# A two-layer graph network on one core: eight units of the adjacency loaded ahead, fourteen moved by transposing DMA, reloads issued from SP

## What is computed

```python
h = relu(layernorm(x))
support = relu(quant(h) @ quant(weight_norm))
x = x + adj @ quant(support)                 # first layer ("layer 0")
h = relu(layernorm(x))
A = (adj + adj.T) * 0.5 + I
dinv = rowsum(A) ** -0.5                     # 0 where the sum is not positive
y = adj @ (dinv[:, None] * A * dinv[None, :])
x = x + y @ h                                # second layer
```

## Time and profile before

| | us |
|---|---|
| median of 3 runs | 505.09 (504.79 to 523.74) |
| the profiled execution, its own time | 509.47 |
| span of that execution, first to last instruction | 507.7 |
| TensorE busy in the span | 489.5 (96%) |
| VectorE, ScalarE, GpSimd busy | 275.9, 142.7, 36.5 |
| mean granted TensorE clock | 0.997 |

### The profile page before, as it was taken

One profiled execution on the slowest core, in us unless ns is written; L12 is line 12 of the kernel. 1 busy time (PEld: TensorE's weight loads), 2 busy tenths in 40 slices (PEclk: granted clock), 3 DMA queues, 4 the chain that ended last, 5 costly groups with the idle time before them and its releaser, 6 DMA issues.

```text
span 507.7 us, 6439 instructions
## 1 busy us (share of the span) xinstructions
PE 489.5 (96%) x2446; PEld 242.4 (48%) x2446; DVE 275.9 (54%) x368; ACT 142.7 (28%) x199; POOL 36.5 (7%) x51
## 2 busy tenths in 40 slices
PE   1899999997999999999999999999999999999997
PEld 1756555553564444444444444444444444444446
DVE  4964779896979878787798767450001000100000
ACT  1885852434544153444432121240000000000000
POOL 1325511132000000000000000000000000000000
PEclk9999999998999999999999999999999999999999
DMA  8970577999934043323224332018001000010001
GB/s 293 402 298 1 187 167 207 196 168 211 305 117 146 0 125 105 102 94 113 83 83 126 104 103 83 0 48 304 21 22 41 21 21 21 21 41 21 21 21 43
DMA packets 39948, 56.89 MB, mean 112 GB/s; under 512 B 22904, under 2 KB 23160, under 8 KB 39928
## 3 DMA queue, kind: packets, MB, share of 16 engines
q1 hardware_dynamic: 37040, 46.15, 30.6%
q10 hardware_dynamic: 2888, 10.49, 7.4%
HBM read 42.99 MB, written 8.39 MB: 101 GB/s over the span
## 4 chain that ended last, share of the span: by engine, by line
PE 84%; DVE 7%; DMA 4%; ACT 2%; issue 1%; SPq 1%; POOL 0%; ACTq 0%
PE ps_a L1098 31%; PE ps_p L997 14%; PE ps_p L1061 7%; PE ps_a L1061 7%; PE ps_b L1061 7%; PE ps_m L1061 4%; PE ps_h L1061 4%; DMA feat<-in_x 2%; DMA at<-at 2%; PE ps_b L979 1%; PE ps_b L951 1%; PE ps_m L997 1%; PE ps_h L997 1%; PE ps_a L979 1%; DVE at L801 1%; DVE small L849 1%
## 5 line engine op out<-in xcount | busy, mean ns | idle before, releaser
L997 PE MATMUL ps_p<-small,at 128*128 128x512 f16 x448 | 102.6, 384 | 2.8 <-DMA at<-at 2.8
L920 DVE SCALAR_TENSOR_TENSOR feat<-ps_a,feat 128x512 f32<-128x512 f32 (+1 forms) x16 | 10.8, 675 | 148.7 <-PE ps_a L1098 144.2
L1098 PE MATMUL ps_a<-small,at 128*128 128x512 f16 x360 | 80.1, 379 | 0.0
L1098 PE MATMUL ps_a<-a_in,at 128*128 128x512 f16 x360 | 80.1, 379 | 0.0
L997 PEld LDWEIGHTS ps_p<-small,at 128*128 128x128 f16 x448 | 44.1, 99 | 52.2 <-issue 5.6
L499 ACT ACTIVATE split<-a_in 128x1024 f16<-128x1024 f32 x30 | 31.7, 1057 | 101.8 <-PE ps_p L1061 90.0
L1098 PEld LDWEIGHTS ps_a<-a_in,at 128*128 (+1 forms) x360 | 35.2, 98 | 42.5
L1098 PEld LDWEIGHTS ps_a<-small,at 128*128 (+1 forms) x360 | 35.2, 98 | 42.5
L845 DVE TENSOR_TENSOR split<-a_in,split 128x1024 f16<-128x1024 f32 x30 | 36.7, 1225 | 34.0 <-ACT split L499 34.0
L1061 PE MATMUL ps_p<-feat,split 128*128 (+1 forms) x180 | 43.9, 379 | 0.5 <-DVE small L849 0.5
L1061 PE MATMUL ps_a<-feat,split 128*128 (+1 forms) x180 | 43.7, 379 | 0.0
(11 more groups left out here) (178 smaller groups left out, 445.0 us busy)
## 6 DMA issues: line engine op xcount, KB each, us to landing
a_in<-in_adj SPq DMA_DIRECT2D x34, 512.0 KB, 3.7
a_in<-in_adj ACTq DMA_DIRECT2D x20, 512.0 KB, 5.0
out<-feat SPq DMA_DIRECT2D x31, 256.0 KB, 2.5
feat<-in_x SPq DMA_DIRECT2D x8, 512.0 KB, 11.3
at<-in_adj SPq DMA_DIRECT2D x8, 512.0 KB, 14.1
feat<-out SPq DMA_DIRECT2D x4, 1024.0 KB, 9.6
at<-in_L_gnn_weight SPq DMA_DIRECT2D x2, 512.0 KB, 3.8
split<-in_adj SPq DMA_DIRECT2D x1, 512.0 KB, 15.8
```

The lines of the kernel that those rows point to most:

```text
L920: nc.vector.scalar_tensor_tensor(out, products, 1.0 / (SA * SZ), out, ALU.mult, ALU.add).then_inc(y_out, 1)
L997: last = nc.tensor.matmul(l0_bank(r), at_block(r, lo, j), small[:, j * D:(j + 1) * D], start=(j == 0 and lo == 0), stop=(j == T - 1 and lo ...
L1098: last = nc.tensor.matmul(BANK[n], at_block(t, lo, j), z_part(j, z_lo), start=(j == 0 and lo + z_lo == 0), stop=(j == T - 1 and lo == 1))
```

## The change

- `MOVED` becomes the fourteen odd units from 3 to 29. Units 3, 5, 27 and 29 are no longer turned. `ADDED` is 1 and these fourteen. Unit 29 gets a stage of its own place in tile 15.
- `AHEAD` becomes 20. Units 12 to 19 are loaded ahead into tiles 10 to 13 of `at`: 16 and 17 into tile 12 once the row transposes are done, 18, 19, 12 and 13 into tiles 13 and 10 once the support products are done, 14 and 15 into tile 11 once the support clamps are done. The ring of `a_in` starts again with unit 20.
- SP issues all loads of `adj`. ScalarE issues none.
- Moves run one step further ahead: step 1 moves units 7 and 9, step `r` from 2 to 11 moves unit `2r + 7`; units 3 and 5 are moved ahead of step 1. Writing a tile from 6 to 13 of `at` now waits until the two units that were loaded into it are done with (`waited_in`), in `move`, `hi_turned` and `lo_turned`.
- The row sums of units 0, 1, 2 and 4 come earlier on ScalarE. GpSimd's first addition waits for `hT_ready` instead of `sq_ready`.

The core of the diff:

```diff
-AHEAD = 12
+AHEAD = 20
-MOVED = tuple(range(7, 26, 2))
-ADDED = (1, 3) + MOVED
+MOVED = tuple(range(3, 30, 2))
+ADDED = (1,) + MOVED
...
         def stage(u, lo):
+            if u == 29:
+                return late(15, 2048 + lo * W, W, f16)
...
+        def in_tile(u):
+            return u // 2 + 4
+        def waited_in(u):
+            return 2 * (u // 2) - 8, 2 * (u // 2) - 7
         def unit_in(u):
             if RING <= u < AHEAD:
-                return late((9, 8, 7, 6)[(u - RING) // 2], u % 2 * 2 * W, W, f32)
+                return late(in_tile(u), u % 2 * 2 * W, W, f32)
...
-        TURNS = {r: [2 * r + 4] for r in range(2, 11)}
-        TURNS.update({1: [4, 5, 6], 11: [26, 27], 12: [28, 29, "acc"], 13: [30, 31]})
-        ROW_SUMS = {4: [0, 1], 5: [2, 3], 6: [4, 5], 8: [6, 8], "acc": []}
-        MOVES = {r: [2 * r + 5] for r in range(1, 11)}
+        TURNS = {r: [2 * r + 4] for r in range(2, 12)}
+        TURNS.update({1: [4, 6], 12: [28, "acc"], 13: [30, 31]})
+        ROW_SUMS = {2: [0, 1], 4: [2, 4], "acc": []}
+        MOVES = {r: [2 * r + 7] for r in range(2, 12)}
+        MOVES[1] = [7, 9]
...
             def move(u):
                 for lo, ready in ((0, hi_ready), (1, lo_ready)):
                     sp.wait_ge(ready, MOVED.index(u) + 1)
-                    if u == 13:
-                        free_slot(sp, 10 + lo)
+                    if u == 29:
+                        wait_moved(sp, 25)
+                        wait_moved(sp, 27)
+                    elif u >= 12:
+                        free_slot(waited_in(u)[lo])
...
-            for u in range(2, AHEAD):
-                rows(sp, u)
+            for u in range(2, 12):
+                rows(u)
             sums(0)
             sums(1)
+            sp.wait_ge(hT_ps, T // 2)
+            rows(16)
+            rows(17)
+            move(3)
+            sp.wait_ge(sup_ps, T // 2)
+            for u in (18, 19, 12, 13):
+                rows(u)
+            sp.wait_ge(sq_ready, T // 2)
+            rows(14)
+            rows(15)
+            move(5)
+            for u in range(AHEAD, AHEAD + 4):
+                rows_again(u)
             for r in range(1, 12):
-                for u in MOVES.get(r, []):
+                if r >= 8:
+                    rows_again(2 * r + 9)
+                for u in MOVES[r]:
                     move(u)
+                if r >= 8:
+                    rows_again(2 * r + 8)
                 store_x1(r - 1)
...
                 if k == 0:
-                    pool.wait_ge(sq_ready, T // 2)
+                    pool.wait_ge(hT_ready, T // 2)
...
             scale_support(4)
             scale_support(5)
+            hi_rows(3)
             scale_support(6)
             scale_support(7)
             hi_turned(2)
-            hi_turned(3)
+            hi_rows(5)
+            for w in ROW_SUMS[2]:
+                row_sum(w)
             for r in range(1, 14):
                 for u in TURNS[r]:
                     if u == 28:
-                        wait_moved(act, MOVED[-2])
-                        wait_moved(act, MOVED[-1])
+                        wait_moved(act, 25)
+                        wait_moved(act, 27)
+                    elif u == 30:
+                        wait_moved(act, 29)
...
                     if u == TURNS[r][0]:
-                        for w in MOVES.get(r - 1, []):
-                            if w > AHEAD:
-                                rows_again(w + RING)
...
                         row_sum(w)
-                        if w < 4 or 12 <= w < UNITS - 4:
-                            rows_again(w + (AHEAD if w < 4 else RING))
...
             clamp_rows(7)
+            lo_rows(3)
             clamp_support(6)
             clamp_support(7)
             lo_turned(2)
-            lo_turned(3)
+            lo_rows(5)
...
             layer0(0, [14, 15])
-            turn(3)
```

More of the change, by code:

```diff
@@ L116, in turn_no @@
             if u == "acc":
-                return turn_no(29) + 1
-            return TURNED.index(u) + (u > 29)
+                return turn_no(28) + 1
+            return TURNED.index(u) + (u > 28)
         def turn_bank(u):
@@ L270, in wait_moved @@
                 engine.wait_ge(at_moved[k % 2][lo], 16 * (k // 2 + 1))
[L272 to L284, removed]
         def arrivals(u):
@@ L293, in load_x, with rows, rows_again, free_slot @@
                 sp.dma_start(feat3[:, 2 * n:2 * n + 2, :], x_tiles[:, 2 * n:2 * n + 2, :]).then_inc(x_in[n], 16)
+            def rows(u):
+                sp.dma_start(unit_in(u), adj[(u // 2) * P:(u // 2 + 1) * P, (u % 2) * W:(u % 2 + 1) * W])\
+                  .then_inc(arr_sem(u), 16)
+            def rows_again(u):
+                free_slot(before(u))
+                rows(u)
+            def free_slot(u):
+                if u in ADDED:
+                    sp.wait_ge(acc_done, ADDED.index(u) + 1)
+                if u in MOVED:
+                    sp.wait_ge(lo_ready, MOVED.index(u) + 1)
+                else:
+                    sp.wait_ge(turned, turn_no(u) + 1)
+                    sp.wait_ge(rs_done, TURNED.index(u) + 1)
             def move(u):
@@ L315, in _ @@
                 load_x(n)
-            rows(sp, 0)
-            rows(sp, 1)
+            rows(0)
+            rows(1)
             for n in range(2, T // 2):
                 load_x(n)
-            for u in range(2, AHEAD):
-                rows(sp, u)
+            for u in range(2, 12):
+                rows(u)
             sums(0)
             sums(1)
+            sp.wait_ge(hT_ps, T // 2)
[4 more added lines that the diff above has]
+            for u in (18, 19, 12, 13):
+                rows(u)
+            sp.wait_ge(sq_ready, T // 2)
[4 more added lines that the diff above has]
+                rows_again(u)
             for r in range(1, 12):
-                for u in MOVES.get(r, []):
+                if r >= 8:
+                    rows_again(2 * r + 9)
+                for u in MOVES[r]:
                     move(u)
+                if r >= 8:
+                    rows_again(2 * r + 8)
                 store_x1(r - 1)
             for v in range(2, 6):
-                free_slot(sp, UNITS - 6 + v)
+                free_slot(UNITS - 6 + v)
                 sums(v)
@@ L428, in row_sum @@
                 nc.scalar.activation(unit_in(u), unit_in(u), ACT.Copy, accum_out=rowsum[:, u:u + 1]).then_inc(rs_done, 1)
-            def rows_again(u):
-                free_slot(act, before(u))
-                rows(act, u)
             def hi_rows(u):
@@ L445, in hi_turned @@
                 act.wait_ge(turned, turn_no(u) + 1)
-                if u == 12:
-                    act.wait_ge(rs_done, TURNED.index(10) + 1)
+                if 12 <= u < 28:
+                    act.wait_ge(rs_done, TURNED.index(waited_in(u)[0]) + 1)
                 nc.scalar.activation(at_half(u // 2, 0, u % 2), turn_bank(u)[:, :], ACT.Copy, scale=SA)\
@@ L533, in _ @@
                     if u == 28:
-                        wait_moved(act, MOVED[-2])
-                        wait_moved(act, MOVED[-1])
+                        wait_moved(act, 25)
+                        wait_moved(act, 27)
+                    elif u == 30:
+                        wait_moved(act, 29)
                     if u != "acc":
                         hi_turned(u)
-                    if u == TURNS[r][0]:
-                        for w in MOVES.get(r - 1, []):
-                            if w > AHEAD:
-                                rows_again(w + RING)
                     if u == TURNS[r][0]:
@@ L661, in lo_turned, with lo_rows @@
                 dve.wait_ge(athi, TURNED.index(u) + 1)
-                if u == 12:
-                    dve.wait_ge(acc_done, ADDED.index(11) + 1)
-                    dve.wait_ge(lo_ready, MOVED.index(11) + 1)
+                if 12 <= u < 28:
+                    dve.wait_ge(acc_done, ADDED.index(waited_in(u)[1]) + 1)
+                    dve.wait_ge(lo_ready, MOVED.index(waited_in(u)[1]) + 1)
                 nc.vector.scalar_tensor_tensor(at_half(u // 2, 1, u % 2), turn_bank(u)[:, :], SA,
                                                at_half(u // 2, 0, u % 2), ALU.mult, ALU.subtract).then_inc(atlo, 1)
+            def lo_rows(u):
+                dve.wait_ge(hi_ready, MOVED.index(u) + 1)
+                nc.vector.scalar_tensor_tensor(stage(u, 1), unit_in(u), SA, stage(u, 0), ALU.mult, ALU.subtract)\
+                  .then_inc(lo_ready, 1)
             def scales():
@@ L797, in turned_out @@
                     lo_turned(u)
[L799 to L802, removed]
             dve.wait_ge(zeroed, 1)
@@ L974, in turn @@
                     pe.wait_ge(atlo, turn_before(u))
-                if u in (2, 3):
-                    pe.wait_ge(sup_out, T // 2 - 3 + u)
+                if turn_no(u) in (2, 3):
+                    pe.wait_ge(sup_out, T // 2 - 3 + turn_no(u))
                 source = acc if u == "acc" else unit_in(u)
```

## The result

| | before | changed |
|---|---|---|
| median of all runs beside each other | 508.03 (503.54 to 523.74, 6 runs) | 511.46 (510.53 to 513.39, 6 runs) |
| ratio | 1 | 1.0125, interval 1.0087 to 1.0164 |
| the profiled execution | 509.47 | 510.96 |
| its span | 507.7 | 509.2 |
| mean granted clock | 0.997 | 0.993 |

The kernel before scatters: three of its six runs took 511 to 524 us. Measured again beside the experiments its median was 504.27 (31 runs), 504.29 (18) and 504.96 (29), with single runs to 520. The ratios are made without the slow runs, those over 1.5% above the fastest of the same kernel. The changed kernel does not scatter: 510.4 to 513.4 in ten runs. It is slower than the kernel before, clear of the interval, and by less than 2%.

A forecast was written before the change was run, and what follows sets the result against it. TensorE was taken to bound the kernel. Fewer turns, a 5.5 us new wait, 0.9 us of clock and no late loss put `layer0(14)` 2.2 us earlier; 505.09 - 2.2 + 4.65 = 507.5 us, range 500.5 to 513.

The forecast's parts named there:

- the landing of `move(5)`: Front of layer 0: behind eight loads and four transposes in SP's one queue, unit 5's move lands at 54.8 us.
- GpSimd beside the low halves: In the chain before `layer0(3)`: GpSimd's adds hold VectorE's two low halves from SBUF, 2.4 us together.
- the clock at half its price: Behind the new wait: half clock costs TensorE 0.9 us, half of the 1.85 seen before, bounds 0 and 1.85.
- the late reload at nothing: Later steps of layer 0: no cost entered for late reloads; the sum took steps 1 to 7 to have none.
- The turns: TensorE in layer 0: units 3, 5, 27 and 29 no longer turned, 3.46 us less work; 18 turns plus `acc`.
- The new wait: TensorE before `layer0(3)`, released by VectorE's x1 after `hi_rows(9)` waits for `move(5)`: about 5.5 us.
- Rivals A: Front hidden: `move(5)` lands by about 51.5 us, `layer0(3)` does not wait; 497 to 501.6 us; chance 0.14.
- rivals B: Transposes mixed with loads cost more, 2.9 us each instead of 1.26; 511 to 517 us; chance 0.12.
- The chance wait: TensorE at 117.10 us waits 2.80 us for a transposing DMA; 4.65 us lost with the clock, taken as gone.
- second reading of the median: Timed runs of the kernel before do have the late wait, so the changed kernel would take 502.9 us.
- Rival C: Steps 8 to 11: the late wait stays, 4.65 us come back; 507.5 to 512 us; chance 0.08.
- The clamps: Support clamps beside GpSimd's earlier first add: cost nothing or one add, 2.45 us, absorbed by the chain; none taken.

## Why the prediction was right in the mechanism, and wrong in the size

The steps that failed are terms of the sum: the landing of `move(5)`, GpSimd beside the low halves, the clock at half its price, and the late reload at nothing. With them a forecast of +0.5% became a measured +1.25%, 511.46 us instead of 507.5.

- **The turns.** Right: 18 turns and that of `acc`.
- **The new wait.** Right in place, chain and releaser.
- **The landing.** Mis-sized, and hidden by luck. Forecast 54.8, measured 55.2. But SP's first load went out at 36.39, 1.3 us earlier than the forecast had it, because the whole front ran earlier. That is chance: the end of the row transposes moves by 2.0 us over the profiles of this case, and by 1.2 us between the two of the kernel before. From the first issue to the landing it was 18.8 us instead of 17.1, and 18.9 to 19.3 to the start of `hi_rows(9)` in both profiles of this kernel and in those with short and with late additions. So eight loads and four transposes in one queue took 1.7 us more than the sum of lone ones; which of them took longer is open. It is far from 2.9 us for each transpose. Rivals A and B fall.
- **GpSimd beside the low halves.** The mechanism was right, the term too small. I had 2.4 us for two low halves; it measured 5.89 - 2.26 = 3.6. The strict case that I had worked out beside it (a request of GpSimd's ahead of the second half, so that this waits for a whole addition) is nearer: 1.2 + 2.35. Two halves in a row, and GpSimd with no gap: 5.89 and 5.74 us in two profiles of this kernel, 6.58 with the later additions; 4.50 where GpSimd had a gap.
- **The clock.** The term was halved for no reason in the rows: the only long wait in the trace before had cost 1.85. It measured 1.82 here, 2.85 in the second profile, and 1.7 to 2.85 in every profile where the clock fell. That is 0.9 us more than the sum had.
- **The late steps.** The chance wait is gone, as assumed. The sum had nothing for the reload of unit 28. In SP's order it stands behind the low half of `move(27)`, which waits for VectorE until late in the step, and what is queued behind it is late with it. 142.14 is 0.56 us late, and 143.53 another 0.51: 1.1 us. This too is partly chance: the second profile has no such wait.
- **Together** 1.7 + 1.2 + 0.9 + 1.1 = 4.9 us, of which the early front took back 1.3: the profiled 507.3 of the sum became 510.96. In the second profile, 510.40, the late reload cost nothing and the clock 1.0 us more. The median of the timed runs lies another 0.5 us above the first profile.
- **The range.** 511.46 lies above the 502.5 to 510.5 that the prediction gave to this mechanism alone. Its own upper terms (a wait of 7.8 us, the clock at 1.85) come to 510.7, and the lower ones with the second reading of the median to under 500, so that range was too narrow at both ends. The number falls where rivals B and C stood, but neither happened.
- **The clamps.** A clamp beside an addition does wait, 5.09 us for two. It was absorbed, as said. Once the long wait is gone it shows: 1.16 us in the versions with unit 9 in step 2.
- **Rival C.** Does not happen. The rule of the Trainium skill beside it would have the reloads on SP's queue cure nothing. In the kernel before with its reloads on SP, and no move further ahead, there was no late wait; see below.
- **A slip in the reading.** GpSimd has three additions more (15 units in `ADDED` instead of 12), not two. The sum did not use this.

## What to carry to other kernels

When a wait is added to an in-order engine, list what is queued behind it and price the whole chain to the engine that bounds, with its accidents (the port, the clock) at the value that the rows show, not at half. A stage that is double buffered should be asked for no sooner than it can be free: handling one unit one step later gave back 9 us, with the same loads, transposes and additions. A wait of a microsecond or so that one profile shows should be looked for in a second one before it is explained. And work that is put into an idle stretch of a queue delays the small urgent transfer behind it; put the urgent one in front, or have nothing wait for it.

## What the runs showed of the hardware that was not expected

- **Two queues against one.** In the kernel before, transposes and loads from two issuers landed in 9.8 us (7.0 in a second profile) at the median; from SP alone 5.1. The Trainium skill ("DMA: Bandwidth & Descriptors", section "Issuing engines are not separate DMA queues") says that DMAs of all issuers run on the same 16 engines, and that issuing from several saves only issue time. Here the landing changed, for nearly the same traffic, though with the loads at other places in the order; the measurement decides. The usual time of the kernel did not change (ratio 0.9975, interval 0.9940 to 1.0010), its scatter did. Why a mixture is slower was not tried.
- **The port.** A low half with two SBUF inputs waits for the end of GpSimd's addition, and so does a clamp: a `tensor_scalar` from SBUF to SBUF, two of which took 5.09 us beside additions and 1.13 with the additions cut short. The Trainium skill ("SBUF — State Buffer", section "Who interferes with whom") names both kinds, the second where it runs in a two-port mode. The runs agree that both wait; the mode in which the clamp ran no profile shows.
- **The clock.** It fell to 0.50 behind waits of 1.99, 2.80, 4.04, 6.95, 6.97 and 8.27 us, and stayed at 1.00 behind 1.16, 1.40, 1.59 and 1.76. The products behind lost 1.7, 1.9, 2.4, 2.9, 1.8 and 2.8 us, with no order in the length of the wait: 6.95 and 6.97 us, in two profiles of one kernel, cost 2.85 and 1.82. With the long wait filled by products of constants they lost nothing.
